# Two-stage convolution and rotation on one core: four granules kept in SBUF, tap tables picked in half-array pairs, and an earlier switch to the steady order

## The reference

```python
# x: (16, 128, 64, 64); 5x5 depthwise kernel with 16 non-zero taps (8 weights, each used with + and -)
def _gn(v, G=32, eps=1e-05):               # group norm: groups of 4 channels, no affine part
    g = v.reshape(B_, G, C_ // G, H_, W_)
    m = jnp.mean(g, axis=(2, 3, 4), keepdims=True)
    s = jnp.var(g, axis=(2, 3, 4), keepdims=True)
    return ((g - m) / jnp.sqrt(s + eps)).reshape(v.shape)

x = x + _L0_conv_ref(_gn(x), L0_conv_weight)              # depthwise 5x5, padding 2
x = x + jnp.einsum('hvc,bchw->bvhw', R[:64], _gn(x))      # one 128x128 rotation per image row h
return x
```

## Time and profile before

| what | before |
|---|---|
| time, median of 3 runs | 479.38 us (477.69 to 479.73) |
| profiled execution, its own time | 481.52 us |
| its span | 479.7 us |
| TensorE busy | 423.4 us, 88% |
| VectorE busy | 361.2 us, 75% |
| ScalarE, GpSimd busy | 275.8 us, 232.5 us |
| DMA moved | 139.03 MB, mean 290 GB/s |
| SP's DMA queue (q1) / ScalarE's (q10), share of the 16 DMA engines | 77.2% / 23.9% |

### The profile page before, as it was taken

One profiled execution on the slowest core, in us unless ns is written; L12 is line 12 of the kernel. 1 busy time (PEld: TensorE's weight loads), 2 busy tenths in 40 slices (PEclk: granted clock), 3 DMA queues, 4 the chain that ended last, 5 costly groups with the idle time before them and its releaser, 6 DMA issues.

```text
span 479.7 us, 8931 instructions
## 1 busy us (share of the span) xinstructions
PE 423.4 (88%) x3225; PEld 224.6 (47%) x3225; DVE 361.2 (75%) x734; ACT 275.8 (57%) x537; POOL 232.5 (48%) x300
## 2 busy tenths in 40 slices
PE   6989979999999999999999999519999877777772
PEld 6544435555555555555555555314444333333330
DVE  5579999999999999999899976715776444555452
ACT  2356645757666576675575675316777654556530
POOL 5446646767566675766566661014444342333310
PEclk9999999999999999999999999857999998999978
DMA  9999979999989999999999999969999999999998
GB/s 166 194 175 233 250 179 253 239 252 239 253 225 234 255 235 240 243 212 254 220 246 251 249 325 305 340 97 370 416 410 413 414 415 419 416 416 416 416 406 302
DMA packets 177587, 139.03 MB, mean 290 GB/s; under 512 B 137608, under 2 KB 139656, under 8 KB 173448
## 3 DMA queue, kind: packets, MB, share of 16 engines
q1 hardware_dynamic: 158280, 105.16, 77.2%
q10 hardware_dynamic: 19264, 33.30, 23.9%
HBM read 71.32 MB, written 67.12 MB: 289 GB/s over the span
## 4 chain that ended last, share of the span: by engine, by line
PE 64%; DMA 22%; DVE 11%; issue 1%; SPq 0%; ACT 0%; DVEq 0%
PE ps L643 51%; DMA out_dram<-area 19%; PE ps L748 9%; DVE stats L539 3%; PE ps L677 3%; DVE area L614 2%; DMA x_scratch<-area 2%; DVE stats L546 2%; DVE area L531 1%; DVE area L528 1%; DVE dev L583 1%; DMA area<-x_scratch 1%; PE ps L661 0%; PE ps L653 0%; DVE area L604 0%
## 5 line engine op out<-in xcount | busy, mean ns | idle before, releaser
L643 PE MATMUL ps<-area 64*64 64x496 f32 (+2 forms) x2560 | 280.2, 588 | 4.0 <-issue 2.6
L643 PEld LDWEIGHTS ps<-area 64*64 64x64 f32 x2560 | 142.8, 133 | 94.7 <-issue 92.8
L342 POOL TENSOR_TENSOR area<-mask,area 128x325 f32<-128x325 f32 x128 | 130.8, 1045 | 62.0 <-PE ps L643 39.6
L748 PE MATMUL ps<-area 128*128 128x512 f32 x256 | 121.2, 623 | 32.0 <-DVE area L614 21.3
L614 DVE TENSOR_TENSOR area<-ps,area 128x512 f32<-128x512 f32 x128 | 82.1, 686 | 65.5 <-DMA out_dram<-area 45.7
L461 ACT ACTIVATE area<-area,norm 128x256 f32<-128x256 f32 x157 | 80.6, 588 | 66.3 <-PE ps L748 55.7
L438 ACT ACTIVATE area<-area,affine 128x256 f32<-128x256 f32 x189 | 96.4, 588 | 34.0 <-DVE affine L561 34.0
L384 POOL TENSOR_SCALAR area<-area,norm 128x256 f32<-128x256 f32 x95 | 51.8, 558 | 122.1 <-PE ps L748 90.4
L415 ACT ACTIVATE area<-ps 64x512 f32<-64x512 f32 x128 | 75.7, 591 | 42.0 <-PE ps L643 39.5
L748 PEld LDWEIGHTS ps<-area 128*128 128x128 f32 x256 | 49.0, 199 | 93.0 <-issue 56.5
L539 DVE BATCH_NORM_STATS2 stats<-area 128x6 f32<-128x512 f32 x128 | 80.3, 689 | 5.6 <-DMA area<-in_x_dram 5.6
(11 more groups left out here) (38 smaller groups left out, 90.1 us busy)
## 6 DMA issues: line engine op xcount, KB each, us to landing
area<-in_x_dram SPq DMA_DIRECT2D x252, 128.0 KB, 4.4
x_scratch<-area ACTq DMA_DIRECT2D x62, 512.0 KB, 6.4
out_dram<-area SPq DMA_DIRECT2D x15, 2048.0 KB, 17.7
area<-x_scratch SPq DMA_DIRECT2D x28, 1024.0 KB, 14.3
area<-x_scratch SPq DMA_DIRECT2D x4, 896.0 KB
out_dram<-area SPq DMA_DIRECT2D x2, 1024.0 KB, 7.8
x_scratch<-area SPq DMA_DIRECT2D x3, 256.0 KB, 6.5
area<-in_x_dram ACTq DMA_DIRECT2D x4, 128.0 KB, 4.1
```

What stands on the lines that cost most here:

```text
L342: last = nc.gpsimd.tensor_tensor(taps[k % TRING][:, c * KW:(c + 1) * KW].rearrange("p d (b r) -> p d b r", r=TAPS), bass.AP(tensor=of_rows ...
L643: last = nc.tensor.matmul(ps[half, bank + c].rearrange("p (j w) -> p j w", j=J)[:, :, outs], taps[k % TRING][rows, (2 * pair + c) * KW + d ...
L748: nc.tensor.matmul(ps[:, m % 6, :], rot_t[u % TURNED][:, h], gn[n % NRING][:, h], start=True, stop=True).then_inc(rotated, 1)
```

## The change

1. **Resident granules.** Image rows 0 to 15 of images 0 to 7 (partitions 0 to 15 of every result group; four granules) are no longer stored to DRAM and loaded again. SP writes them into SBUF, one DMA per channel: 16 partitions of 2 KB each are gathered in one partition (`keep_rows`). Four such DMAs follow the eight loads of each step in SP's queue. The store on ScalarE's queue shrinks to the other 112 partitions and becomes one DMA. The slots of stage 2 grow from 9 to 11 (four kept, seven of the x ring).
2. **Handover.** The seven other first granules (4 to 10) are loaded in two parts, channels 0 to 63 early and 64 to 127 once all groups are stored. Granules 0 to 3 wait for no load, only for the kept rows. The stage's last `add` on VectorE moves ahead of two small operations; the matmuls that pick the norms of the last groups are split, 6 of 8 ahead of the last average; three rotation units are turned ahead instead of two. Granules are taken in another order at the beginning (0 to 3 from images 0 to 7, 4 to 7 from images 8 to 15, the same rows).
3. **Tap tables.** They are built on both 64-partition halves. Chunks become 16, 32, 32, 32, 16 channels; of each chunk's five picks, the low half of the array does two and the high half three, in turn. The 16 column writes become 6. Four chunks come ahead of the first average, one behind it.
4. **FILL is 2** instead of 4.
5. **First loads.** One of the four DMAs for the second half of group 0 moves from ScalarE's queue to SP's, and ScalarE's queue takes the second half of group 1.

```diff
-CHUNKS = ((0, 16), (16, 48), (48, 88), (88, C))
+CHUNKS = ((0, 16), (16, 48), (48, 80), (80, 112), (112, C))
+CHUNK_ROWS = (range(0, 2), range(2, TAPS))
+CHUNK_BANKS = ((1, 2), (3, 4), (5, 0), (1, 2), (3, 4))
-FILL = 4
+FILL = 2
-EXTRA = 2
-IRING = XRING + EXTRA
+KEPT = 4
+KEPT_ROWS = KEPT * RH
+IRING = XRING + KEPT
+FIRST_CHANNELS = 64
+        def y_free(queue, k):
+            queue.wait_ge(x1_stored[k % YRING], 16 * (k // YRING))
+            queue.wait_ge(x1_kept[k % YRING], 16 * GC * (k // YRING))
+        def store(queue, k, cs):
+            dst = x1_dram[k * GC + cs.start:k * GC + cs.stop].rearrange("c n h j w -> (n h) c (j w)")
+            queue.dma_start(dst[KEPT_ROWS:P], y[k % YRING][KEPT_ROWS:P, cs]...)
+        def keep_rows(queue, k, cs):
+            for c in range(cs.start, cs.stop):
+                queue.dma_start(kept[k * GC + c:k * GC + c + 1].rearrange("p h j w -> p h (j w)"),
+                                y[k % YRING][0:KEPT_ROWS, c].rearrange("p j w -> p (j w)")
+                                ).then_inc(x1_kept[k % YRING], 16)
...
+            for s in range(GROUPS + 1):
+                if s >= 2:
+                    sp.wait_ge(x1_ready, 2 * (s - 1))
                 if group(s + XRING - 2) and s >= 1:
                     load_half(sp, s + XRING - 2, 0)
                     load_half(sp, s + XRING - 2, 1)
+                if s >= 2:
+                    keep_rows(sp, s - 2, slice(0, GC))
...
+                    if s >= GROUPS - 1:
+                        load_granule(n, slice(0, FIRST_CHANNELS))
+                        if s == GROUPS - 1:
+                            for m in range(KEPT, n):
+                                load_granule(m, slice(0, FIRST_CHANNELS))
+            for pair in range(2):
+                sp.wait_ge(x1_ready, 2 * GROUPS - 1 + pair)
+                keep_rows(sp, GROUPS - 1, slice(2 * pair, 2 * pair + 2))
+                store(sp, GROUPS - 1, slice(2 * pair, 2 * pair + 2))
+            load_granule(IRING - 1, slice(0, FIRST_CHANNELS))
             groups_stored(sp, GROUPS)
-            load_part(2)
+            for n in range(KEPT, IRING):
+                load_granule(n, slice(FIRST_CHANNELS, C))
...
-            load_half(act, 0, 1)
+            load_half(act, 0, 1, range(GC - 1))
+            load_half(act, 1, 1)
...
-            dve.wait_ge(in_landed[0], granule_landings(0))
+            rows_kept(dve)
...
+                for i in range(len(CHUNK_ROWS[1])):
+                    for half, rows, bank in zip((low, high), CHUNK_ROWS, CHUNK_BANKS[n]):
+                        if i < len(rows):
+                            done = nc.tensor.matmul(ps[:, bank, i * end:(i + 1) * end],
+                                                    row_pick[half, rows[i]].rearrange("p n h -> p (n h)"),
+                                                    col_taps[half, :, first:last], start=True, stop=True)
```

More of the change, by code:

```diff
@@ L165, in conv_rotate_kernel @@
         x1_stored = [sem(f"x1_stored{n}") for n in range(YRING)]
+        x1_kept = [sem(f"x1_kept{n}") for n in range(YRING)]
         norm2_stored = sem("norm2_stored")
@@ L210, in conv_rotate_kernel, with load_half @@
         STEPS = range(-3, GROUPS + 3)
-        def load_half(queue, k, n):
-            for c in range(GC):
+        def load_half(queue, k, n, cs=range(GC)):
+            for c in cs:
                 queue.dma_start(xin[k % XRING][n * HALF:(n + 1) * HALF, :, c],
@@ L225, in groups_stored @@
+        def keep_rows(queue, k, cs):
[3 more added lines that the diff above has]
+                                ).then_inc(x1_kept[k % YRING], 16)
         def groups_stored(queue, groups):
             for k in range(YRING):
-                done = len(range(k, groups, YRING))
-                queue.wait_ge(x1_stored[k], 32 * done + (32 if groups == GROUPS and k == (GROUPS - 1) % YRING else 0))
@@ L230, in store @@
-        def store(queue, k):
-            queue.wait_ge(x1_ready, 2 * (k + 1))
-            for n in range(2):
-                rows = slice(n * HALF, (n + 1) * HALF)
-                dst = x1_dram[k * GC:(k + 1) * GC, n].rearrange("c h j w -> h c (j w)")
-                queue.dma_start(dst, y[k % YRING][rows].rearrange("p c j w -> p c (j w)")
-                                ).then_inc(x1_stored[k % YRING], 16)
-        def tap_batches():
-            banks = iter((1, 2, 3, 4, 5, 0, 3, 4, 5))
-            for n, (first, last) in enumerate(CHUNKS):
-                per = 512 // (KW * (last - first))
-                for row in range(0, TAPS, per):
-                    yield n, first, last, range(row, min(row + per, TAPS)), next(banks)
+                queue.wait_ge(x1_stored[k], 16 * groups_through(k, YRING, groups)
+                              + (16 if groups == GROUPS and k == (GROUPS - 1) % YRING else 0))
@@ L245, in _, with rows_kept @@
+        def rows_kept(queue):
+            for k in range(YRING):
+                queue.wait_ge(x1_kept[k], 16 * GC * groups_through(k, YRING, GROUPS))
+        def tap_batches():
+            batches = [(chunk, *CHUNKS[chunk], rows, bank) for chunk in range(len(CHUNKS))
+                       for rows, bank in zip(CHUNK_ROWS, CHUNK_BANKS[chunk])]
+            return batches
         @block.sync
@@ L688, in _ @@
             pe.wait_ge(col_taps_ready, 2)
-            pick_taps(1)
-            pick_taps(2)
+            for n in range(1, 4):
+                pick_taps(n)
             for half in (low, high):
@@ L717, in _ @@
                     pe.wait_ge(own_ready, 2 * GROUPS - 1)
-                    turn_rotations(0)
-                    turn_rotations(1)
+                    for u in range(PAIR + 1):
+                        turn_rotations(u)
                 for at, d in enumerate(OFFSETS):
```

221 lines of the change are left out of this document (120 added, 101 removed).

## The result

The change made the kernel slower, by far more than the gain that was forecast. Median of four runs 549.39 us (544.83 to 555.05) beside 479.56 us for the kernel before (four runs, 477.69 to 485.97) on the same chip. Ratio 1.140 [1.134, 1.147], without the slowest run of either kernel, in which the chip was in its slower state. The profiled execution took 546.80 us, its span is 545.0 us. Forecast were 471 us, 459 to 503; **the result is outside the range and on the other side of no change.** It lies near the upper end of rival A, the kept rows that jam the engines (554).

A forecast was written before the change was run, and what follows sets the result against it. Stage 1 was taken as bound by TensorE and by the DMA queues, stage 2 by DMA. From 479.7 us, 4.1 by the convolution's end and 4.5 for handover and stage 2 gave 471.1, so 471 us; range 459 to 503.

The forecast's parts named there:

- rival A: Stage 1: kept rows jam the DMA engines in few partitions; slower, 497 us at 1.2 us a batch, 554 at 3.6; chance 0.27.
- SP's issue: Stage 1, SP's queue: four kept DMAs of some 0.4 us and eight loads of 0.64 fit into 8.66 us.
- the bounds for the engines: Stage 1, kept rows: nothing to 3.6 us added a batch; 0.13 taken, +1.2 us after the room.
- the room stays: Stage 1, x loads: they come as much earlier as TensorE does, so the room stays 1.2 + 0.75 us.
- Start: Kernel start, tap tables and first loads: first convolution at about 14.5 us instead of 18.0, -3.45 us.
- the tables: Start, tap tables: a chunk costs three slots instead of five picks, 1680 columns, 6.5 us; before, picks took 8.47 us.
- as before: Start, first loads: x of group 0 is measured by 10.9 us, the same as in the kernel before.
- Rival C: Start brings less: picks do not overlap or first measurement arrives later; -1.5 instead of -3.45, 473 to 475 us; chance 0.12.
- FILL: Filling order of stage 1: the long interval between reciprocals comes at once, later ones are shorter; -1.9 us.
- Handover and stage 2: From the convolution's end to the kernel's end: all stored at about 318, end at 475.2 in the clock of before, -4.5 us.
- the rate of half-width loads: Handover: loads into 64 partitions cost 5.4 us a MiB, near 200 GB/s, twice the price of full width.
- rival B: Handover: half-width loads cost little with 8 KB packets, 2.56 us a MiB, second halves 9.0 instead of 18.9 us; 461; chance 0.13.

The follow-up runs named there:

- run 7: Changed kernel with the four kept DMAs a group, still on SP's queue, moving 64 B of each row instead of 2 KB into a scratch tile: 506.4 us.
- run 2: Changed kernel with each channel's kept rows written into sixteen partitions instead of one, on the same queue: 515.0 us.
- run 4: Changed kernel with the kept rows of groups 0 to 30 issued by ScalarE behind each store instead of by SP: 520.3 us.
- run 5: Changed kernel with the kept rows both spread over sixteen partitions and issued by ScalarE: 474.1 us.
- run 6: Changed kernel, kept rows on ScalarE's queue, a group's four partitions 32 apart: 497.2 us. Readings: single partitions limit too; or partitions 32 apart share a limit.
- run 9: Changed kernel with kept rows on ScalarE's queue, four neighbouring partitions, but only 1 KB of each 2 KB row: 472.5 us.
- run 13: Kernel before with only a group's two stores of 64 partitions made one of 128: ratio 0.9895.
- run 1: Kernel before with the changed tap tables, first loads and FILL 2, nothing of the residency: ratio 0.997.
- run 15: Run 10 with FILL 4 as before instead of FILL 2: ratio 0.985.
- Run 3: Changed kernel with the kept rows' DMAs left out, GpSimd filling their place once: 470.2 us.
- Run 10: As run 1 (kernel before with new tap tables, first loads, FILL 2), plus a group's two stores made one DMA of 128 partitions: ratio 0.981.
- run 8: As run 1, plus channels 0 to 95 of two more granules loaded early behind the last store: ratio 1.011 to the kernel before.

## Why the prediction was wrong

**The step that failed first** is the sentence "SP's issue (four more of some 0.4 us to eight of 0.64) fits into 8.66 us". The 0.64 for x loads was right (5.42 / 8 = 0.68 with the pauses between them, where nothing jams); the 0.4 had no row of its own, and 0.6 was measured. With 0.6 it would still fit: 5.42 and the 2.49 of the handover's four make 7.9 us. What it left out is that the kept DMAs right behind eight x loads are drawn out, to 2.1 us (run 7) and 2.9 us (run 2). The four take 3.7 to 4.9 us, whatever their bytes, and SP's queue needs about 10 us a group, over 8.66. Run 7 puts this alone at 29 us. I had bounded the engines' cost of these transfers from both sides, and the issuing queue's not at all.

**The second** is the choice inside the bounds for the engines. Ends were nothing and 3.6 us a batch; I took 0.13, because the first 8 KB an engine of the 12-partition loads had passed almost at the usual price. What these packets cost themselves was indeed little: in run 4 the packets of q10, kept rows and store together, took 95 ns in the mean (34.4% of 16 engines in 160 us, 9253 packets) beside 92 in run 5, where nothing jams (39.4%, 10980). The price is paid by the x packets in the other queue: 34 ns in run 4 (89.5%, 66971), 25 in run 5 (75.1%, 78000). So run 4, with SP out of it, takes 10.0 us a group beside 8.66, and ends 46.8 us late. The rest of that row, 108 GB/s at a share of 89%, was the part that counted. It pointed to the upper end.

By the Trainium skill (SBUF — State Buffer, Door 1: The DMA port swizzle) four neighbouring partitions share a port of 27.2 GB/s, and partitions 32 apart lie on the same one. An estimate from this figure: a batch of 128 KiB holds its port for 4.8 us. The trace of the changed kernel agrees nearly: its engines moved 35 and 37 GB/s in the two jammed microseconds shown above. By the same map run 4 writes to one port at a time, run 6 to two and run 5 to four, and they end their convolution 46.8, 20.4 and 2.1 us late. This agrees too, and it favours the second reading of run 6. Half the bytes (run 9) cost almost nothing, for which no run has the reason. The net loss measured is smaller, 1.3 us a group in run 4 (10.0 beside 8.66); an engine need not be held for the whole batch and some of it had cover, but no run parts the two. Rival A with this rule stood at 554 us, the result is 549; but that agreement is luck in part, because A knew nothing of SP's queue. Run 4, where the engines alone hold the loads, took 520.

**Rival A**: right in sign and place, and in size by luck; of its signs, waits for x of 5 us and more and steps over 8.7 us both came. **The missing term**: the merged store was costed at nothing. It is worth 5.0 us alone (run 13), and it let the x loads follow an earlier start, for which I had claimed "the room stays". Without it they could not (run 1).

**Start**: the tables were right (picks 6.24 us, forecast 6.5). The first loads were named with them and then treated as if x of group 0 came "as before". It came 1.2 us later; with the old loads the first convolution is at 14.8, forecast 14.5. Rival C had this. **FILL**: mechanism and spacing right, size 1.9 forecast, 3.4 measured at the convolution's end (run 15).

**Handover and stage 2**: the rate of half-width loads was right (199 GB/s, forecast near 200) and rival B wrong. From the convolution's last matmul to the end of the span the forecast, in its clock of before, is 475.2 - 303.4 = 171.8 us. Run 3 takes 169.4, run 5 171.1, the changed kernel 183.5. Without the jam the size was about right, but that is no proof of its terms. The terms up to the point where everything is stored are said to reach 318 and add up to 315.7 (289.9 and 25.8), and the 1 us of receipt among them has no row. And the merged store, which is not among them, brings this stretch to 170.0 us by itself, without any residency (run 13; the rotation starts 14.5 us behind the convolution, before 20.9). With the kept rows I missed that the last of them, in the queue behind the half-width loads, now release the rotation: 16.3 us. The period of stage 2 is unchanged at 414 GB/s, as taken.

The sum without its wrong terms was near: the span was forecast at 471.1, and run 3 has 468.4, run 5 472.2. A good part of that is luck. Run 10 has the new start, FILL 2 and one store a group, but no residency and no new handover, and its span is 469.4. So the store, which had no term, brought what the forecast expected of the terms of handover and stage 2.

## What to carry to other kernels

Cost a new transfer three times: bytes on the engines, time of the issuing queue (with what DMAs ahead of it add), and where it lands. When many engines write into few partitions, ask what stands behind their packets, for that is where the bill goes, and here little of it showed (1.2 us in run 9) until the group's total passed the period of TensorE. Of two DMAs that cover half of the partitions each, make one; it was the best single edit here. An earlier start is worth nothing if the loads that feed it have no room; look for that room first. And before you make data resident, measure what the smaller edits of the same change give by themselves: here they gave all but about 1 us.

## What the runs showed that I had not expected

- A DMA from SBUF to SBUF with 16 rows takes 0.6 us of SP's queue to issue, with 32 KB or with 1 KB, about as long as an x load of 128 KB (0.64). Right behind eight x loads one or two of four take 1.3 to 2.9 us, also with the engines' share at 0.73 to 0.79 (runs 7 and 2). Why is open: no run put fewer x loads ahead of them.
- Merging two 64-partition stores lowered the share of their own queue by 18% (42.2% to 34.7% of the engines for nearly the same bytes), raised that of the x loads, and left the sum a MB as it was (2.65% and 2.72%).
- While loads into 96 of 128 partitions ran (run 8), with some small ones among them, the engines moved 158 to 266 GB/s at a share of 89 to 115%, nearer to the 199 of 64 partitions than to the 414 of all.
